# Another order of the attention's three engines on three and three PSUM banks, with 16 groups of transposes in a head

## What is computed

```python
mod = (_silu(c) @ wmod).reshape(1, 6, 1, -1)          # sa, ca, ga, sb, cb, gb
h = _layernorm(x) * (1 + ca) + sa
k, q, v = (einsum('ihd,bpd->biph', W, h) for W in (W_K, W_Q, W_V))
scores = einsum('biph,biqh->biqp', k, q)              # causal mask, softmax over p, / sqrt(128)
z = einsum('biqp,biph->biqh', attn, v)
x = x + ga * einsum('df,bqf->bqd', W_O, z_flat)
h = _layernorm(x) * (1 + cb) + sb
x = x + gb * ffn(h)                                   # 4-bit weights, silu(gate) * up, RMS norm
```

## Time and profile before

| | us |
|---|---|
| median of 3 runs | 2062.76 (2061.78 to 2062.84) |
| the profiled execution | 2062.91 |
| its span | 2061.1 |
| TensorE busy | 2042.0 (99%), 12077 products |
| VectorE busy | 1377.0 (67%) |
| ScalarE busy | 1049.3 (51%) |
| GpSimd busy | 800.3 (39%) |
| mean granted clock of TensorE | 0.999 |
| attention | 214.5 to 1597.4 |
| a steady head | 86.31 |

### The profile page before, as it was taken

The page is one execution under the profiler, slowest core; times in us unless marked ns, Lnnn a source line. Parts: engine busy times, 40 slices in busy tenths (PEclk is TensorE's granted clock), DMA queues, the critical chain, the costliest instruction groups (busy, mean ns, idle before and its releaser), DMA issues. The chain is left out here.

```text
span 2061.1 us, 37203 instructions
## 1 busy us (share of the span) xinstructions
PE 2042.0 (99%) x12077; PEld 1801.0 (87%) x12077; DVE 1377.0 (67%) x3107; ACT 1049.3 (51%) x1962; POOL 800.3 (39%) x591
## 2 busy tenths in 40 slices
PE   9999999999999999999999999999999999999998
PEld 8888899999999999999999999999998788788787
DVE  5453667676676766766667565665656677799998
ACT  4422455555455555555555555555555343588732
POOL 2030437254362533625336100000009444488776
PEclk9999999999999999999999999999999999999999
DMA  8885321212212122221212201012024676101322
GB/s 271 234 248 185 92 72 51 88 51 63 71 57 84 54 64 64 63 79 58 64 59 69 75 22 56 28 46 64 25 58 155 228 249 225 67 31 42 126 78 76
DMA packets 174484, 195.40 MB, mean 95 GB/s; under 512 B 13751, under 2 KB 120010, under 8 KB 174154
## 3 DMA queue, kind: packets, MB, share of 16 engines
q1 hardware_dynamic: 172105, 190.27, 29.8%
q10 hardware_dynamic: 2304, 4.20, 0.5%
HBM read 124.03 MB, written 70.40 MB: 94 GB/s over the span
## 5 line engine op out<-in xcount | busy, mean ns | idle before, releaser
L1250 ACT ACTIVATE pT_hi<-ps_t 128x512 fp32r<-128x512 f32 (+3 forms) x640 | 303.5, 535 | 244.0 <-PE ps_t L1176 241.9
L1335 DVE TENSOR_TENSOR pT_lo<-ps_t,pT_hi 128x512 fp32r<-128x512 f32 (+3 forms) x640 | 356.1, 604 | 57.7 <-ACT pT_hi L1250 56.3
L1258 ACT ACTIVATE probs<-probs,rmin 128x128 f32<-128x128 f32 (+15 forms) x256 | 309.3, 1210 | 162.6 <-DVE rmin L1326 162.1
L208 PE MATMUL ps_z<-pT_lo,v_hi 128*128 128x256 f32 (+1 forms) x1152 | 325.0, 282 | 0.0
L209 PE MATMUL ps_z<-pT_hi,v_lo 128*128 128x256 f32 (+1 forms) x1152 | 324.7, 282 | 0.0
L207 PE MATMUL ps_z<-pT_hi,v_hi 128*128 128x256 f32 (+1 forms) x1152 | 317.8, 276 | 0.8 <-DVE pT_lo L1335 0.8
L1176 PE MATMUL ps_t<-ident,probs 128*128 128x128 f32 x2176 | 283.4, 273 | 0.1
L1176 PEld LDWEIGHTS ps_t<-ident,probs 128*128 128x128 f32 x2176 | 245.5, 140 | 9.1 <-ACT probs L1258 0.5
L207 PE MATMUL ps_s<-kq 128*128 128x512 f32 (+3 forms) x640 | 247.1, 386 | 2.4 <-PEq L356 1.1
L209 PE MATMUL ps_s<-kq 128*128 128x512 f32 (+3 forms) x640 | 231.1, 361 | 0.0
L208 PE MATMUL ps_s<-kq 128*128 128x512 f32 (+3 forms) x640 | 230.5, 360 | 0.0
(11 more groups left out here) (214 smaller groups left out, 4324.3 us busy)
## 6 DMA issues: line engine op xcount, KB each, us to landing
scratch_v<-p_vo_hi SPq DMA_DIRECT2D x64, 256.0 KB, 2.9
scratch_v<-p_x SPq DMA_DIRECT2D x64, 256.0 KB, 3.5
v_hi<-scratch_v SPq DMA_DIRECT2D x64, 256.0 KB, 3.5
v_lo<-scratch_v SPq DMA_DIRECT2D x64, 256.0 KB, 4.0
scratch_zT<-z SPq DMA_DIRECT2D x256, 64.0 KB, 1.7
w_raw<-in_w_qkv SPq DMA_DIRECT2D x16, 512.0 KB, 3.9
tile_z<-scratch_zT SPq DMA_DIRECT2D x14, 512.0 KB, 6.9
tile_scales<-scratch_recips SPq DMA_DIRECT2D x14, 512.0 KB, 7.9
```

What stands on the lines that cost most here:

```text
L208: nc.tensor.matmul(dst, stat[0], mov[1], start=False, stop=False)
L1250: nc.scalar.activation(pT[0][:, slot, i % 2, 0:w], ps_t[:, (chunks_before(i) + u) % T_BANKS, 0:w], ACT.Copy).then_inc(t_hi, 1)
L1258: nc.scalar.activation(probs[:, i % 2, 0:w], probs[:, i % 2, 0:w], ACT.Exp, bias=rmin[:, i % 2:i % 2 + 1], scale=-1.0, accum_out=sums[:, i ...
L1335: nc.vector.tensor_tensor(pT[1][:, slot, i % 2, 0:w], ps_t[:, (chunks_before(i) + u) % T_BANKS, 0:w], pT[0][:, slot, i % 2, 0:w].bitcast(F ...
```

## The change

The three lists PE_ORDER, ACT_ORDER and DVE_ORDER are replaced by others with the same entries and the same shifts. Nothing else is changed: the same banks, buffers, waits and tails. In the new list of TensorE transposes stand in 16 groups (17 before), five of which are followed directly by a product of probabilities and values. Rows are taken up in the same sequence, but transposes, scores and values of different rows interleave otherwise.

```diff
--- before.py
+++ after.py
@@ -81,25 +81,26 @@
 
 
 PE_ORDER = """
-    S0.0 S1.0 S2.0 T15.0- T15.1- T15.2- S3.0 PQ1.0 Z7.0- T15.3- PQ1.1 PQ1.2 PQ1.3 Z7.1- Z7.2- Z7.3- N0- T0.0 T1.0 S4.0
-    PK2.0 S4.1 S5.0 Z0.0 T2.0 T3.0 PK2.1 PK2.2 S5.1 PK2.3 Z1.0 T4.0 T4.1 S6.0 PQ2.0 PQ2.1 PQ2.2 PQ2.3 S6.1 T5.0 T5.1
-    S7.0 S7.1 PK3.0 PK3.1 PK3.2 PK3.3 Z2.0 Z2.1 T6.0 T6.1 T7.0 S8.0 S8.1 S8.2 T7.1 PQ3.0 Z3.0 S9.0 PQ3.1 Z3.1 S9.1
-    S9.2 T8.0 T8.1 T8.2 S10.0 S10.1 S10.2 PQ3.2 PQ3.3 T9.0 T9.1 T9.2 S11.0 S11.1 S11.2 Z4.0 Z4.1 Z4.2 T10.0 T10.1
-    T10.2 S12.0 S12.1 S12.2 PQ0.0+ T11.0 T11.1 T11.2 PQ0.1+ S12.3 S13.0 Z5.0 Z5.1 Z5.2 S13.1 S13.2 S13.3 T12.0 T12.1
-    T12.2 S14.0 S14.1 T12.3 S14.2 PQ0.2+ PQ0.3+ S14.3 T13.0 T13.1 T13.2 S15.0 S15.1 PK0.0+ Z6.0 Z6.1 Z6.2 T13.3 T14.0
-    T14.1 PK0.1+ PK0.2+ Z6.3 PK0.3+ S15.2 S15.3 T14.2 T14.3 PK1.0+ PK1.1+ PK1.2+ PK1.3+
+    S0.0 T15.0- T15.1- T15.2- S1.0 S2.0 S3.0 PQ1.0 T15.3- PQ1.1 Z7.0- PQ1.2 T0.0 T1.0 Z7.1- PQ1.3 Z7.2- Z7.3- T2.0
+    T3.0 PK2.0 S4.0 N0- PK2.1 S4.1 PK2.2 S5.0 PK2.3 S5.1 S6.0 S6.1 Z0.0 T4.0 T4.1 PQ2.0 PQ2.1 PQ2.2 PQ2.3 S7.0 Z1.0
+    T5.0 T5.1 T6.0 PK3.0 PK3.1 S7.1 S8.0 PK3.2 PK3.3 Z2.0 T6.1 T7.0 T7.1 Z2.1 S8.1 S8.2 PQ3.0 PQ3.1 S9.0 S9.1 PQ3.2
+    S9.2 T8.0 T8.1 T8.2 Z3.0 PQ3.3 S10.0 S10.1 S10.2 Z3.1 T9.0 T9.1 T9.2 S11.0 S11.1 Z4.0 S11.2 T10.0 T10.1 T10.2 Z4.1
+    Z4.2 S12.0 S12.1 S12.2 T11.0 T11.1 S12.3 PQ0.0+ S13.0 PQ0.1+ S13.1 Z5.0 T11.2 T12.0 S13.2 Z5.1 S13.3 S14.0 T12.1
+    T12.2 T12.3 S14.1 PQ0.2+ PQ0.3+ S14.2 Z5.2 S14.3 S15.0 PK0.0+ S15.1 T13.0 T13.1 PK0.1+ PK0.2+ PK0.3+ S15.2 T13.2
+    T13.3 T14.0 Z6.0 S15.3 Z6.1 Z6.2 T14.1 T14.2 T14.3 PK1.0+ Z6.3 PK1.1+ PK1.2+ PK1.3+
 """
 ACT_ORDER = """
-    E0 H15.0- H15.1- H15.2- H15.3- E1 UQ1 G0- Y7- H0.0 H1.0 E2 E3 Y0 H2.0 H3.0 E4 UK2 E5 Y1 H4.0 H4.1 UQ2 H5.0 H5.1 E6
-    E7 UK3 Y2 H6.0 H6.1 H7.0 H7.1 E8 Y3 H8.0 H8.1 H8.2 E9 UQ3 H9.0 H9.1 H9.2 E10 E11 Y4 H10.0 H10.1 H10.2 H11.0 H11.1
-    H11.2 E12 Y5 H12.0 H12.1 H12.2 E13 H12.3 UQ0+ H13.0 H13.1 H13.2 E14 H13.3 H14.0 H14.1 Y6 UK0+ H14.2 H14.3 E15 UK1+
+    E0 H15.0- H15.1- H15.2- H15.3- E1 H0.0 E2 E3 UQ1 H1.0 H2.0 G0- Y7- UK2 E4 H3.0 H4.0 E5 Y0 UQ2 H4.1 E6 H5.0 H5.1
+    H6.0 Y1 E7 UK3 H6.1 H7.0 Y2 E8 H7.1 H8.0 H8.1 H8.2 E9 Y3 H9.0 UQ3 H9.1 E10 H9.2 H10.0 H10.1 E11 H10.2 H11.0 Y4
+    H11.1 E12 H11.2 H12.0 H12.1 H12.2 H12.3 UQ0+ E13 E14 H13.0 Y5 H13.1 UK0+ H13.2 H13.3 H14.0 H14.1 H14.2 E15 H14.3
+    Y6 UK1+
 """
 DVE_ORDER = """
-    C0.0 UK1 L15.0- L15.1- L15.2- C1.0 L15.3- UQ1 C2.0 C3.0 L0.0 L1.0 X0 C4.0 L2.0 L3.0 C4.1 C5.0 C5.1 UK2 C6.0 L4.0
-    L4.1 C6.1 UQ2 L5.0 L5.1 C7.0 C7.1 UK3 L6.0 L6.1 L7.0 C8.0 X1 L7.1 C8.1 C8.2 C9.0 C9.1 C9.2 L8.0 L8.1 L8.2 C10.0
-    C10.1 C10.2 UQ3 L9.0 L9.1 L9.2 C11.0 C11.1 C11.2 X2 L10.0 L10.1 L10.2 C12.0 C12.1 L11.0 L11.1 L11.2 C12.2 C12.3
-    C13.0 C13.1 C13.2 C13.3 L12.0 L12.1 L12.2 C14.0 C14.1 L12.3 C14.2 C14.3 UQ0+ L13.0 L13.1 L13.2 C15.0 L13.3 L14.0
-    L14.1 C15.1 UK0+ C15.2 C15.3 L14.2 L14.3 R0
+    C0.0 UK1 L15.0- L15.1- L15.2- C1.0 L15.3- C2.0 L0.0 C3.0 X0 UQ1 C4.0 L1.0 L2.0 C4.1 C5.0 C5.1 UK2 C6.0 L3.0 L4.0
+    C6.1 UQ2 L4.1 L5.0 L5.1 C7.0 C7.1 L6.0 UK3 L6.1 C8.0 C8.1 C8.2 L7.0 X1 L7.1 C9.0 C9.1 C9.2 L8.0 C10.0 L8.1 L8.2
+    C10.1 C10.2 L9.0 C11.0 C11.1 L9.1 L9.2 C11.2 UQ3 L10.0 L10.1 C12.0 C12.1 L10.2 C12.2 L11.0 C12.3 L11.1 X2 C13.0
+    C13.1 C13.2 L11.2 L12.0 C13.3 L12.1 C14.0 C14.1 UQ0+ C14.2 L12.2 C14.3 L12.3 L13.0 L13.1 C15.0 C15.1 L13.2 L13.3
+    UK0+ C15.2 C15.3 L14.0 L14.1 L14.2 R0 L14.3
 """
```

## The result

The changed kernel takes 2065.95 us (median of 14 runs, 2064.16 to 2068.19), the kernel before 2061.76 (14 runs, 2059.68 to 2062.88). The ratio is 1.002, with an interval of 1.0012 to 1.0027: slower by about 4 us, some 0.2%. The profiled execution of the changed kernel took 2067.42 us, the third longest of its runs, with a span of 2065.6. Its lines in the code are one higher than before (L1335 is L1336).

The account below looks back on a forecast made before the run. TensorE's own instruction stream was taken to bound the kernel. 2062.9 us plus 0.5 (switches), 1.2 (first head) and 0.75 (last head and barrier) gave 2065.35, or 2065.2 beside the median; range 2061.0 to 2071.0.

Parts of the forecast that it names:

- Steady waits: 0: Heads 1 to 14: no TensorE stall, each wait covered by 0.4 us or more of TensorE work.
- the margins of 0.5 us at T4.0 and Z4.0: Steady head: row 4's exponent ready 0.5 us before T4.0 needs it, T9.0's low part 0.5 before Z4.0.
- Switches: +0.5 us: TensorE's changes of product kind: +0.03 us a head, bounds -0.16 and +0.25, so +0.5 us for 15 heads.
- The lower count as a rival: Fewer transposition-to-score/projection changes save 0.16 us a head, 2.9 us under forecast: 2062.3; chance 0.08 shared with clock regained.
- First head: +1.2: First head: waits for exponents of rows 2 and 3 and UQ1's low part lose 2.4 us instead of 1.2.
- Last head, TensorE's end: +1.6: Last head: some 2.9 us lost, including row 13's low parts, so TensorE's end comes 1.6 us later.
- GpSimd at the barrier: -0.8: Barrier behind the attention: GpSimd's last scaling ends about 0.8 us earlier, making TensorE the last.
- The net term +0.75: Last head and barrier: TensorE ends at 1598.1 against GpSimd's 1597.3 before, net +0.75 us.
- Behind the barrier: 0: Output projection behind the barrier: the forecast's sum holds no term for it.
- the third rival: Lower switch count, 2062.3; with the clock kept up behind the barrier, 1.6 us less, 2060.7; chance 0.08 for either.
- The prediction's last sentence: Attention: a wait for a DMA there would mean that SP's order was misjudged.
- the likeliest case: Whole kernel: time within 0.2% (4.1 us) of the old one, called the same, chance 0.69.

Follow-up runs that it names:

- the last experiment: Changed kernel with TensorE's list rearranged for 15 entries, old lists in first and last head, VectorE doing the last half scaling: 2057.74 us against 2061.91, ratio 0.9982.
- the old first head: Changed kernel, but head 0 runs the three old lists: 2065.63 us, ratio 1.0015 to the kernel before.
- the two edits together: Changed kernel with the last head's first output tile copy moved later and W_O's part 3 issued before pair 3's store: 2063.15 us, ratio 1.0006 to the kernel before.

## Why the prediction was right, and where it was not

The forecast of 2065.2 (2061.0 to 2071.0) stands beside 2065.95, and the likeliest case, within 0.2% (4.1 us), beside +4.19 between the medians: just over that bound. The sum came out by the right mechanism in two terms, and in the others partly by chance.

- *Steady waits: 0.* Right. No wait is listed in heads 1 to 14; the margins of 0.5 us at T4.0 and Z4.0 held.
- *Switches: +0.5 us.* Too much: +0.02. What failed is the price list. I charged 0.023 for an entry behind transpositions, 0.018 behind values and 0.01 for a change between scores and projections. The last is nothing: those 10 ns were, as far as the spacings tell, the recovery behind the entry, which I counted a second time. Counted as entries the two lists have 21 and 22, and twenty extra ones cost 11.6 ns each. The changes from transpositions to values, five in a head, which no row showed, cost nothing in 14 heads.
- *The lower count as a rival* had TensorE gain 0.16 us a head. It did not. In the last experiment a head is 0.12 shorter with fewer entries and fewer narrow ends before scores, so a list can gain in this way.
- *First head: +1.2.* Measured +0.86, by the waits that I named: 0.9 for exponents and 0.6 for q, in place of 1.1.
- *Last head, TensorE's end: +1.6.* With the clock up it is +1.41 (94.84 against 93.43), with the waits where I put them, 1.86 and 0.41 on row 13's low parts and 0.5 more. What I left out is the clock: in the changed kernel's trace it fell behind those waits, and TensorE's end moved 1.37 us further, to 96.21.
- *GpSimd at the barrier: -0.8.* This step failed. It ended 3.64 us later. I saw that tile 0 is stored and loaded later, and took from it only what the scaling itself loses; I didn't count the load of the weight, which stands behind the tile's two loads on SP's queue. Issuing it earlier gave the 3.64 us back and 0.2 more. The net term +0.75 was 3.64.
- *Behind the barrier: 0.* It was -0.87 in these two traces. Before, TensorE waits 1.1 us for a low part of the output's input, after 0.2. With one profile of each I can say where it lies, not that it is there in each run.
- *The start of the attention: 0.* +0.82, without a cause in the change; 1.2 us is what it varies over the traces.

The sum of the forecast is +2.45 over the profiled execution before; between the two traces it is +4.48. The terms are off by +2.89 (last head to first output product), -0.48 (switches), -0.34 (first head), -0.87 (the rest) and +0.82 (the start), so the total stood nearer than its largest term. Between the medians it is +4.19, and the predicted time looks closer still (0.75 us) because the median before came out 1.0 us lower in 14 runs than in the three that I had. The half clock behind the barrier, priced at 1.6 us in the third rival, costs just that. Right were the bottleneck, the absence of steady stalls and both places in the edge heads; the cause of most of the loss, a transfer in SP's order, was none of my cases. The prediction's last sentence names it as what would prove me wrong, a wait for a DMA in the attention, and that is the line that the trace shows.

**The clock at the barrier** was in the third rival, and its rule held: with TensorE last, the idle time is 1.7 us and the clock stays. Over the eleven traces, idle times at the barrier of 1.7 (four of them) and 2.3 us left the granted clock at 1.00, and those of 2.5 to 5.0 (six) were met by half the clock, for 3.4 us in five of them and for 6.8 behind the 5.0. These are one trace for each kernel, and the clocks of the unprofiled runs with 2.3 us (above) warn against reading a limit from them. From the first output product to the end are 459.0 to 459.5 us without the fall, and 460.7 to 462.5 with it. The fall of 3.4 us is worth 1.6 of that, by the traces without a further wait (459.1 and 460.7); the rest are waits of TensorE behind the barrier, and the longer fall. A wait of 1.86 us with 0.41 close behind it in the last head was met by half the clock in two traces (after, and with the old first head) and not in a third.

The Trainium skill (TensorE: Matmul & The Clock Gate, Part 1: The HAM clock gate) says that how many products run slow at a kernel's start differs from run to run of the same kernel. These traces show the like in a kernel's middle, with the same wait and two outcomes; so a forecast can give such a fall a chance and not a place. The kernel of its section A second HAM failure mode: psum-queue depth-cycling idled briefly between its groups. No run here has such idle times inside a steady head: 115 changes of kind in a head, without a wait, left the clock at 1.00.

The Trainium skill (DMA: Bandwidth & Descriptors, Queues, rings and completion order) has each DMA engine take a ring's descriptors in order. The weight's 256 KB behind 2 MB agree with that: 8.4 us from its issue to landing, right behind the tile's own two loads, which took 6.2 and 8.2; issued ahead of them the same load took 2.6.

**What stays open.** Whether the narrow ends are what makes an entry cost 11.6 ns in one pair of lists and 20 in another; a list with only those moved would show it. How the 4.0 us of the weight's earlier load divide: in the traces 3.1 are there at the first output product and 2.1 come behind it, of which the clock is 1.6 and a wait 0.2, and the fall goes with the longer idle time, so the two weren't had apart. What the last head's wait costs once GpSimd isn't late: the two edits together show 0.3 us at the first output product, and no gain of the median.

## What to carry to other kernels

An order of work that is moved carries its stores and loads with it: go through each DMA queue again, in order, and ask of every transfer what now stands in front of it and which engine waits for it, the one that isn't the bottleneck too, if a barrier is ahead. A list that runs without a stall in the loop's middle has to be costed once more for its first and last turn, where entries are missing. And a barrier's idle time can have two prices, its own and that of the clock behind it: here 0.9 us less of it came with 1.6 us more from the clock in the trace, and with 2.2 us in all between the medians, of which the interval leaves 0 to 3.7.

## Hardware behaviour that was not expected

- Between fp32r products of 512 columns, starts are 0.227 us apart. Twenty more places in a head where such products follow transpositions or values cost 0.23 us, and a change between two kinds of 512-wide products costs nothing.
- At the barrier, idle times of TensorE of 1.7 and 2.3 us left the granted clock at 1.00 (five traces), and behind those of 2.5 us and over it was half for 3.4 to 6.8 us (six traces). A wait of 1.86 us with one of 0.41 close behind it was met by half the clock in two traces of three. 3.4 us at half clock cost 1.6.
- A load of 256 KB issued 0.5 us behind loads of 1.0 and 0.96 MB landed 8.4 us later; issued ahead of them it landed after 2.6.
